# A graph network's node and table stages as one pipeline over blocks, with centred features and weights

## The reference, cut to what matters

```python
x = _layernorm(x + L0(x, ...));  x = _layernorm(x + L1(x, ...))
# L1:
edge_attr = _mlp(_ln(edge_embed, eng, enb), eW1, eb1, eW2, eb2)
for l in range(3):
    h = _ln(x, n1g[l], n1b[l])
    q, kn, vn = h[dst] @ Wq[l] + bq[l], h[src] @ Wkn[l] + bkn[l], h[src] @ Wvn[l] + bvn[l]
    ...                       # alpha: softmax over the edges of a dst, 8 heads
    agg = segment_sum((vn + ve) * alpha)
    gate = sigmoid(agg @ Wih[l] + bih[l] + h @ Whh[l] + bhh[l])
    upd = agg + gate * (h @ Wself[l] + bself[l] - agg)
    x = x + upd @ Wout[l] + bout[l]
    x = x + _mlp(_ln(x, n2g[l], n2b[l]), mW1[l], mb1[l], mW2[l], mb2[l])
return _ln(x, ng, nb)
```

## Time and profile before

| | |
|---|---|
| median of three runs | 9160.3 us (9158.19 to 9160.95) |
| the profiled execution | 9160.98 us; its span 9159.2 |
| busy share | POOL 70%, DVE 63%, PE 40%, ACT 31% |
| mean granted clock of TensorE | 0.686 |
| instructions | 45368 |

### The profile page before, as it was taken

How to read it: one execution, slowest core, us unless ns; L and a number is a source line. 1 busy time by engine, 2 the same in 40 slices (tenths; PEclk the granted TensorE clock), 3 DMA queues, 4 the chain that set the end, 5 groups by cost and what they waited for, 6 DMA issues and landing times.

```text
span 9159.2 us, 45368 instructions
## 1 busy us (share of the span) xinstructions
PE 3667.0 (40%) x9857; PEld 2190.5 (24%) x9857; DVE 5799.7 (63%) x6114; ACT 2862.4 (31%) x2181; POOL 6365.8 (70%) x6734
## 2 busy tenths in 40 slices
PE   2677777776323233223342232322242222223325
PEld 1333333333122122212121221222222122212212
DVE  1666666666366776676437667767744776677673
ACT  0566666666122222222222222222221222222223
POOL 6677777774577777777457777777736777777762
PEclk9988888888656566555666665665576656656557
DMA  3455555554433443444234334434314443444331
GB/s 52 161 192 180 186 179 174 175 184 148 132 131 131 139 149 131 139 140 141 64 108 148 132 132 141 147 131 139 125 49 138 139 149 131 137 141 141 131 110 48
DMA packets 405487, 1247.08 MB, mean 136 GB/s; under 512 B 196101, under 2 KB 253910, under 8 KB 360006
## 3 DMA queue, kind: packets, MB, share of 16 engines
q0 software_dynamic: 215104, 429.19, 17.4%
q1 hardware_dynamic: 169606, 468.24, 14.6%
q10 hardware_dynamic: 20736, 349.23, 9.5%
HBM read 808.34 MB, written 437.84 MB: 136 GB/s over the span
## 4 chain that ended last, share of the span: by engine, by line
POOL 52%; issue 20%; PE 17%; ACT 7%; DVE 2%; DMA 1%; DVEq 1%; ACTq 0%; POOLq 0%; SPq 0%
POOL G L546 49%; PE PS L696 7%; PE PS L689 6%; ACT S L910 4%; POOL qexp L599 1%; PE PS L777 1%; POOL QQ L588 1%; PE PS L781 1%; ACT hid L886 1%; PE PS L666 1%; POOL s2exp L565 1%; POOL S L552 1%; POOL G L588 1%; ACT S L851 0%; ACT L855 0%
## 5 line engine op out<-in xcount | busy, mean ns | idle before, releaser
L546 POOL DMA_INDIRECT G<-tabkv,srcI x4704 | 4438.4, 944 | 1433.6 <-issue 1433.6
L756 PE MATMUL PS<-Wkvp,EA 128*128 128x256 f32 x4704 | 1672.9, 531 | 4296.3 <-DVE PX L1438 4217.8
L756 PEld LDWEIGHTS PS<-Wkvp,EA 128*128 128x128 f32 x4704 | 1253.4, 274 | 4716.5 <-DVE PX L1438 4381.7
L546 POOL DMA_INDIRECT G<-tab,srcI x1568 | 1481.4, 945 | 571.9 <-issue 507.2
L959 ACT ACTIVATE QQ<-QQ 128x3584 f32<-128x3584 f32 x84 | 538.4, 6410 | 3313.5 <-DVE PX L1438 3063.1
L1435 DVE TENSOR_TENSOR PS<-PS,G 128x512 f32<-128x512 f32 x588 | 408.4, 695 | 1593.3 <-DMA G<-tabkv,srcI 1575.3
L973 ACT ACTIVATE S<-SX 128x4480 f32<-128x4480 f32 x81 | 663.7, 8194 | 1238.4 <-DVEq L1462 1238.4
L689 PE MATMUL PS<-xT,W1p 128*128 128x512 f32 x1568 | 768.5, 636 | 252.2 <-ACT xT L847 243.1
L1424 DVE TENSOR_TENSOR_SCAN QQ<-PS,QQ 128x456 f32<-128x456 f32 x672 | 679.4, 1082 | 207.9 <-ACT QQ L959 192.3
L1461 DVE TENSOR_TENSOR_SCAN SX<-PS,SX 128x456 f32<-128x456 f32 x756 | 763.2, 1082 | 12.2
L696 PE MATMUL PS<-hid,W2p 128*128 128x512 f32 x1568 | 710.9, 596 | 34.2 <-ACT hid L886 31.5
(11 more groups left out here) (311 smaller groups left out, 4090.8 us busy)
## 6 DMA issues: line engine op xcount, KB each, us to landing
st<-S ACTq DMA_DIRECT2D x81, 2240.0 KB, 7.8
EA<-eaT SPq DMA_DIRECT2D x84, 1792.0 KB, 7.8
QQ<-qexp SPq DMA_DIRECT2D x84, 1792.0 KB, 7.3
st<-S ACTq DMA_DIRECT2D x27, 3668.0 KB, 12.0
G<-tabkv,srcI POOLq DMA_INDIRECT x4704, 2.5
xe<-in_edge_attr SPq DMA_DIRECT2D x28, 1792.0 KB, 8.1
qexp<-zeros SPq DMA_DIRECT2D x28, 1792.0 KB, 12.6
eaT<-eaC ACTq DMA_DIRECT2D x28, 1792.0 KB
```

The costliest lines, as they stand in the source:

```text
L546: nc.gpsimd.indirect_dma_start(out=G[:, u, t, :], out_offset=None, in_=tab[:, :], in_offset=IND(ap=srcI[:, u, t:t + 1], axis=0)).then_inc( ...
L756: last = mm(PS[:, b + j // 2, 2 * P * (j % 2):2 * P * (j % 2) + 2 * P], EA[:, u, 4 * s + j, :], Wkvp[:, :], start=True, stop=True)
```

## The change

**Pipeline.** `in_turn` sorts all steps of all seven blocks by 8 x block + depth, and PE, ACT and DVE each walk their own part of that one list, with a semaphore of its own for each step. Node stage of layer l and table stage of layer l + 1 are one such list (depths 0 to 28.5), so that the loop becomes: table stage 0, then `Fori(0, L - 1)` of edge pass and joint list, then the last layer written out with `LAST_*` steps (two norms, the way back). Transposes of all blocks go through bank 7, one block at a time. The products with `Whh` for all blocks stand ahead of the list. Each of a block's up to four projection tiles has its own signal and its own two additions on DVE.

**Centring.** `Cmat` is `ident - onesD`. x is centred once by a product, and `Wout`, `mW2` and their biases are centred on DVE at each layer (`centred_weights`), so x stays centred; norms no longer compute or subtract a mean. The inverse root is ACT's `Sqrt` followed by DVE's `reciprocal`, in place of `Ln` and `Exp`.

**SP.** `node_weights(0)` and four loads for the last norm stand in the preamble, ahead of the loop over groups; `node_weights(l + 1)` stands behind the stores of the joint list. Stores go block by block (4 a block). x1 is reloaded into a free buffer (`nX1`) at the start of the last stage.

**First pass.** POOL's hold stands ahead of every second gather (k > 3) rather than every eighth.

```diff
-A_DVE = 3 * NB
-B_PE, B_ACT, B_DVE = 11, 8, 5
-HALVES = (range(0, 3), range(3, NB))
+TILES = NPR
+SKEW = 8
...
+def tiles_to(k):
+    return min(4 * k + 4, TILES)
+def in_turn(depth):
+    order = sorted((SKEW * k + d, k, step) for k in range(NB) for step, d in depth.items())
+    return [(k, step) for _, k, step in order if not (step.startswith("project") and int(step[-1]) * P >= BLK[k][1])]
...
+        nX1 = S1[:, :, :].rearrange("p c r -> p (c r)")[:, 0:NW]
+        NODE_PE = {"turn": 1, "gate": 3, "self": 5, "out": 7, "spread2": 10, "hidden0": 12, "hidden1": 14, "hidden2": 16,
+                   "hidden3": 18, "fold": 20}
+        NODE_ACT = {"agg": 2, "gate": 4, "square2": 9, "root2": 10.5, "relu0": 13, "relu1": 15, "relu2": 17, "relu3": 19}
+        NODE_DVE = {"sums": 0, "mix": 6, "onto": 8, "norm": 11, "onto2": 21}
+        TABLE_PE = {"spread": 23, "project0": 25, "project1": 25.5, "project2": 26.5, "project3": 27.5}
+        TABLE_ACT = {"square": 22, "root": 23.5}
+        TABLE_DVE = {"h": 24, "project0": 26, "project1": 26.5, "project2": 27.5, "project3": 28.5}
+        LAST_PE = {"spread": 23, "y_centre": 25, "y_spread": 27, "y_turn": 29}
+        LAST_ACT = {"square": 22, "root": 23.5, "y_square": 26, "y_root": 27.5}
+        LAST_DVE = {"y": 24, "y_norm": 28, "y_copy": 30}
+        def bank_of(k, j):
+            return k - 1 if k > 0 and j % 2 == 1 else k
...
+            node_weights(0)
+            for q in range(2):
+                for j, name in ((NGC, "ng"), (NBC, "nb")):
+                    sp.dma_start(cb[q * D:(q + 1) * D, j:j + 1], A[name].unsqueeze(1), allow_slow_non_contiguous=True).then_inc(c_x, 16)
...
+            def store_tables1(m):
                 for k in range(NB):
-                    hold(sp, waits_sp, a_dve, l * A_DVE + 2 * NB + k + 1)
+                    hold(sp, waits_sp, projection_used, m * TILES + tiles_to(k))
                     c0, w = BLK[k]
                     sp.dma_start(tabkv[2 * c0:2 * (c0 + w), :].rearrange("(t p) w -> p t w", p=P),
                                  nkv[k % 2][:, 0:2 * w].rearrange("p (t w) -> p t w", w=2 * D)).then_inc(a_out[k % 2], 16)
-                sp.dma_start(hTd[:, :], nH).then_inc(h_out, 16)
-                sp.dma_start(tabq[:, :].rearrange("(t p) d -> p t d", p=P), q_all[:, :, :]).then_inc(q_dram, 16)
+                    sp.dma_start(tabq[2 * c0:2 * (c0 + w), :].rearrange("(t p) d -> p t d", p=P),
+                                 q_all[:, 2 * c0 // P:2 * (c0 + w) // P, :]).then_inc(q_dram, 16)
+                    sp.dma_start(hTd[:, c0:c0 + w], nH[:, c0:c0 + w]).then_inc(h_out, 16)
+                    sp.dma_start(xTd[:, c0:c0 + w], nX[:, c0:c0 + w]).then_inc(h_out, 16)
...
+                if last:
+                    hold(sp, waits_sp, st1_out, (l + 1) * (16 * (NCH + 1)) + 16)
+                    sp.dma_start(nX1, x1Td[:, :]).then_inc(c_x, 16)
+                else:
+                    edge_weights(l + 1)
+                    store_tables1(l + 1)
+                    node_weights(l + 1)
+            store_tables1(0)
+            with sp.Fori(0, L - 1) as l:
+                layer(l, False)
+            layer(L - 1, True)
...
-                    for k in range(PT):
-                        if k > 0:
-                            hold(pool, waits_pool, m_pe, 28 * (2 * i + u - 1) + (4 * k - 3 if k > 1 else 0))
-                        gathers(u, G0, tab0, lambda t: got0[u], range(8 * k, 8 * k + 8))
+                    for k in range(C // 2):
+                        if k > 3:
+                            hold(pool, waits_pool, m_pe, 28 * (2 * i + u - 1) + k - 3)
+                        gathers(u, G0, tab0, lambda t: got0[u], range(2 * k, 2 * k + 2))
...
-                        hold(pool, waits_pool, a_dve, l * A_DVE + 2 * NB + j // 8 + 1)
+                        hold(pool, waits_pool, projection_used, l * TILES + tiles_to(j // 8))
...
+                if step == "turn":
+                    hold(pe, waits_pe, sums_ready, at)
+                    if k > 0:
+                        hold(pe, waits_pe, agg_ready, at - 1)
                     for j in range(w // P):
+                        last = tr(PS[:, 7, j * P:(j + 1) * P], nag[:, c0 + j * P:c0 + (j + 1) * P], ident[:, :])
+                    last.then_inc(turned, 1)
+                elif step == "gate":
+                    hold(pe, waits_pe, agg_ready, at)
+                    mm(PS[:, k, 0:w], Wn[:, 1, :], nB2[:, cols], start=False, stop=True, skip_group_check=True).then_inc(gate_ready, 1)
...
+                    j = int(step[-1])
+                    if j == 0:
+                        hold(pe, waits_pe, h_ready, m * NB + k + 1)
+                    elif j == 1:
+                        hold(pe, waits_pe, projection_used, m * TILES + max(4 * k, 1))
+                    else:
+                        hold(pe, waits_pe, projection_used, m * TILES + 4 * k + (j - 1 if k > 0 else j))
+                    mm(PS[:, bank_of(k, j), 0:6 * D], nH[:, c0 + j * P:c0 + (j + 1) * P], Wqkv[:, :],
+                       start=True, stop=True).then_inc(projected, 1)
...
+                mm(PS[:, 7, 0:2], Cmat[:, :], cb[:, BOUT:MB2 + 1], start=True, stop=True).then_inc(bias_centred, 1)
+                for k in range(NB):
+                    c0, w = BLK[k]
+                    mm(PS[:, k, 0:w], Wn[:, 2, :], nH[:, c0:c0 + w], start=True, stop=False, skip_group_check=True)
...
+                mm(PS[:, k, 0:w], Cmat[:, :], nX[:, c0:c0 + w], start=True, stop=True).then_inc(x0_centred, 1)
+            for k, step in in_turn(TABLE_PE):
+                table(k, step, 0)
...
+                for k, step in in_turn({**NODE_PE, **TABLE_PE}):
+                    if step in NODE_PE:
+                        node(k, step, l)
+                    else:
+                        table(k, step, l + 1)
...
+                elif step == "square2":
+                    act.wait_ge(x_ready, at)
+                    f(nB3[:, cols], nX[:, cols], ACT.Square).then_inc(squared2, 1)
+                elif step == "root2":
+                    act.wait_ge(spread2, at)
+                    f(nB4[:, cols], PS[:, k, 0:w], ACT.Sqrt, bias=epsc[:, 0:1]).then_inc(rooted2, 1)
...
+                act.wait_ge(x0_centred, k + 1)
+                f(nX[:, c0:c0 + w], PS[:, k, 0:w], ACT.Copy)
+                f(nB3[:, c0:c0 + w], PS[:, k, 0:w], ACT.Square).then_inc(squared, 1)
...
+            def scaled_by_spread(k, dst, g_, b_):
+                c0, w = BLK[k]
+                cols = slice(c0, c0 + w)
+                v.reciprocal(nB4[:, cols], nB4[:, cols])
+                settle()
+                tt(nB5[:, cols], nX[:, cols], nB4[:, cols], ALU.mult)
+                settle()
+                return ts(dst[:, cols], nB5[:, cols], cb[:, g_:g_ + 1], cb[:, b_:b_ + 1], ALU.mult, ALU.add)
...
+                    j = int(step[-1])
+                    if j == 0 and k >= 2:
+                        dve.wait_ge(a_out[k % 2], m * (16 * ((NB + 1 - k % 2) // 2)) + 16 * (k // 2))
+                    dve.wait_ge(projected, m * TILES + 4 * k + j + 1)
+                    s_ = PS[:, bank_of(k, j), 0:6 * D].rearrange("p (q w) -> p q w", q=2)
+                    kv_ = nkv[k % 2][:, j * 4 * D:(j + 1) * 4 * D].rearrange("p (q w) -> p q w", q=2)
+                    t = 2 * (c0 // P + j)
+                    tt(kv_, s_[:, :, D:3 * D], bkv[:, :, :].rearrange("p a d -> p (a d)").unsqueeze(1).broadcast_to([P, 2, 2 * D]), ALU.add)
+                    tt(q_all[:, t:t + 2, :], s_[:, :, 0:D], bqkv[:, 0, :].unsqueeze(1).broadcast_to([P, 2, D]), ALU.add)
+                    settle().then_inc(projection_used, 1)
...
+                for q in range(2):
+                    red(wmean[q * D:(q + 1) * D, 0:1], Wn[q * D:(q + 1) * D, 3, q * D:(q + 1) * D], AX.X, ALU.add)
+                    red(wmean[:, 1 + 2 * q:3 + 2 * q], mW2s[:, :, q, q * D:(q + 1) * D], AX.X, ALU.add)
+                settle()
+                ts(wmean[:, 0:5], wmean[:, 0:5], 1.0 / D, None, ALU.mult)
+                settle()
+                for q in range(2):
+                    own = Wn[q * D:(q + 1) * D, 3, q * D:(q + 1) * D]
+                    ts(own, own, wmean[q * D:(q + 1) * D, 0:1], None, ALU.subtract)
+                    own = mW2s[:, :, q, q * D:(q + 1) * D]
+                    tt(own, own, wmean[:, 1 + 2 * q:3 + 2 * q].unsqueeze(2).broadcast_to([P, 2, D]), ALU.subtract)
+                dve.wait_ge(bias_centred, l + 1)
+                cp(cbc[:, :], PS[:, 7, 0:2])
...
+                elif step == "y":
+                    dve.wait_ge(rooted, L * NB + k + 1)
+                    scaled_by_spread(k, nB5, NGC, NBC)
                     settle()
+                    tt(nB5[:, cols], nB5[:, cols], nX1[:, cols], ALU.add).then_inc(h_ready, 1)
+                elif step == "y_norm":
+                    dve.wait_ge(y_rooted, k + 1)
+                    v.reciprocal(nB4[:, cols], nB4[:, cols])
                     settle()
```

(22 more changed lines are left out.)

418 lines of the change are left out of this document (197 added, 221 removed).

## The result

The changed kernel took **9175.0 us** (median of 20 runs, 9172.35 to 9178.97), the kernel before 9161.0 in the same series (20 runs): a ratio of 1.0016, 95% interval 1.001 to 1.0022. So it is 14 us slower, clear of noise but inside the 0.2% called "no change" ahead; 9188 was forecast. The profiled execution has a span of 9173.8 us, 14.6 above that of before.

A forecast was written before the change was run, and what follows sets the result against it. Edge passes were taken as bound by POOL's gathers, so only stretches without gathers could move. Preamble +8, first pass 0, first table stage +4, steps -10, last stage +25 sum to +27: 9188 us, range 9120 to 9250.

The forecast's parts named there:

- the forecast's mixture: Whole kernel: the summed terms with PE's clock between its two levels, 9188 us, own range 9135 to 9225; chance 0.62.
- full clock: Rival: PE stays at full clock in the pipe, projections end at 4665, total -51 us, 9110; chance 0.14.
- table loads at twice the price: Rival: ACT's alternating Sigmoid and Sqrt loads cost as much again beyond 1.28 us, +38, 9226; chance 0.1.
- costly holds: Rival: 18 more POOL holds a chunk at 0.3 us exceed the first pass's slack, +108, 9296; chance 0.05.
- within: Outcome for the whole time: no change, meaning within 18 us of 9160 (0.2%); chance 0.16.
- SP's weights ahead of the indices: Steps between layers: 30 loads (18.5 us) precede the indices, so the next gather comes at 4708.9 against 4714.07, -5 us each.
- The walk through the order: Joint node and table list, walked: block sums 15 to 25 us apart, last projection used at 4686.
- The reciprocal: DVE's norms: 3.35 us over 512 columns, range 2.3 to 4.4; two added per block, 6.7 us.
- the last term: Last stage as one pipe: 216 us from first sums to end instead of 191, +25 (full clock 0, half clock +52).
- the preamble: 34 DMAs of 0.62 us ahead of SP's loop delay POOL's first gather to 103.3: +8 us (7 to 12).
- the second step: Layer 1 to 2, node and table stage to the next pass: -5 us, as in the first step.
- First pass: POOL's holds at every second gather: fulfilled holds cost nothing that shows, 0 us.

The follow-up runs named there:

- the naive repair: Changed kernel with each layer's 30 node-weight loads behind the first chunks' indices and features, preamble's four behind its loop: 10827.7 us, against 10790.2 with only preamble loads moved.
- Ln and Exp: Changed kernel with Ln and Exp of -0.5 on ACT in place of Sqrt and DVE's reciprocal: 10790.5 us, against 10805.6 for the changed kernel.
- the finer stagger: Changed kernel with weights loaded at each pass's end and blocks staggered by 4 steps instead of 8: 10689.8 us, ratio 0.9829 to the kernel before.

## Why the prediction was right

**The balance of many terms.** The forecast said that a large rearrangement nets little, since DVE's own work grows and a wait moves: the first scatter of a step came 81 us earlier, the last 22, the next pass 5.3 and 8.1. Of the cases, the forecast's mixture is the one that came about; full clock (9110), table loads at twice the price (9226) and costly holds (9296) did not. But of the three outcomes, "slower by over 0.2%" had 0.63 and what came, "within", 0.16: 13 of the 27 us forecast are missing, and nearly 8 of them are the last stage.

**SP's weights ahead of the indices**: forecast (213.3 from first sums to first gather) and seen (213.2), with the releaser named. That the two agree to 0.1 us is luck: the list ended 2.0 us earlier than walked, and stores, weights and indices took 25.1 us behind it instead of 22.9. The experiments showed what the naive repair costs.

**The walk through the order**: starts of the seven sums within 2 us, end within 2. It used a clock between the levels; 0.82 was granted. That the clock would lie there was a guess, and it had its bounds for the two levels (4665 and 4735). Two of its terms were off in opposite ways. DVE's 118 us for the list measured 106.9, or some 113 with the short gaps between its own instructions. PE's 14.4 us a block at full clock make 110 us over six and a quarter blocks at 0.82 (an estimate); PE was busy 126.7. So the picture in which everything follows DVE's work is too simple: the waits between engines are more than the 6 us of 25 counted, as Ln and Exp and the finer stagger show.

**The reciprocal**: 3.35 us, from two rows at 8 and 64 columns. The estimate of 4.3 us, worked out from the repeat count of 8 in the Trainium skill, "VectorE: DVE Perf Modes", section "First, the fixed hardware budget", doesn't fit the trace. The Trainium skill, "ScalarE: Activation LUTs", section "What ACT_TABLE_LOAD costs", puts a switch at 2.66 us, of which 1.38 are a drain. The trace agrees with the load, 1.28, but not with the drain: of the 146 loads of the changed kernel 78 begin 0.02 us after the function before them, and the next function mostly starts 0.01 after the load.

**What was off** is the size of the last term, "the walk gives periods of 15 to 22, then 30 ... and 5.5 for store and landing": +17.3 instead of +25. The sums of the last block came at 139.8 and not 146, and the end 2.1 us after the copy instead of 5.5, probably because stores go out block by block and only the small one is left; against that, the first sums came 2.6 later after the row gathers, which no term of the forecast had and whose cause is open. The smaller misses: the preamble (+5.7 for +8; of the 7.1 us of POOL's delay 1.4 came back from two slow gathers that vanished), the second step (-8.1 for -5; its wait for the indices is 1.3 us shorter than in the first step and its list 1.9).

**First pass**: 0 on the first chip, as said; that the same holds gain 0.6 to 0.7% on the slower chips was in no case of the forecast.

## What to carry to other kernels

Before an engine's stage is moved, ask what is queued behind it on the queue that nobody counts: here the pipeline freed POOL 22 us earlier, and 17 of them went to a queue that issues 30 small loads ahead of the one that POOL waits for. Put such loads where their queue is idle, not only behind the urgent ones: with 15 others beside a stream of gathers they held the queries back by 120 us. And a pipeline in fixed order is worth its overlap: the same work with up to seven blocks under way instead of four took 17 to 21 us less of 226. A single profiled step of such a list varied by 9 us with nothing changed in it, so compare two runs before believing a smaller gain.

## What the runs showed of the hardware

- The same program took 9161 us on one chip and 10872 to 10883 on three others, at nearly the same granted clock (0.686 and 0.665). In the edge passes the slower ones show POOL idle ahead of gathers for a cause outside the core's own records ("remote"), 694 us in the 4704 gathers of the kernel before, where the first chip shows none; a gather itself takes 0.944 to 0.946 us on both.
- SP issued a small load every 0.64 us while POOL waited. Beside a stream of gathers on a slower chip it was one every 2.1 to 4.3 us in two passes (75 us for 30 loads in the first), and 34 us for the same 30 in a third. On the first chip 15 loads beside the first gathers of a pass took about 0.65 each.
- A reciprocal on DVE costs about 6.25 ns a column between rows of 8 and 64 columns, 3.35 us over 512 columns and 0.95 over 128; a pass over two operands takes 0.69 us over 512.
